# VectorE copies a pair's turned probabilities before it reduces the pair two further on, in the narrow self-attention of a two-layer decoder

## The reference

```python
def _L0_xattn_ref(x, cross_input, Wk, bk, Wq, bq, Wv, bv, ...):
    # C, H = 128, 16; D = C // H = 8; x is the layer norm of the stream
    q = _heads(x @ Wq + bq)
    k = _heads(x @ Wk + bk)
    v = _heads(x @ Wv + bv)
    att = jnp.einsum('bhqd,bhkd->bhqk', q, k) * scale
    causal = jnp.tril(jnp.ones((T, T), bool))
    att = jnp.where(causal[None, None], att, -jnp.inf)
    y = jnp.einsum('bhqk,bhkd->bhqd', jax.nn.softmax(att, axis=-1), v)
    ...            # cross-attention is added to y
    y = y.transpose(0, 2, 1, 3).reshape(x.shape[0], T, C)
    return y @ Wp + bp
```

## Time and profile before

| | |
|---|---|
| runs | 2798.28 us median of 3 (2797.87 to 2806.37) |
| profiled execution | 2795.5 us, of which the span from first to last instruction is 2793.8 us |
| granted TensorE clock, mean of the span | 0.924 |
| busy in the span | PE 2405.5, PEld 1793.3, DVE 2002.1, ACT 1641.1, POOL 1108.5 us |
| busy from 1000 to 1023 us, about one batch of the narrow stage | PE 22.01, PEld 15.18, DVE 18.34, ACT 18.88, POOL 2.94 us |

### The profile page before, as it was taken

One profiled execution on the slowest core, in us unless ns is written; L12 is line 12 of the kernel. 1 busy time (PEld: TensorE's weight loads), 2 busy tenths in 40 slices (PEclk: granted clock), 3 DMA queues, 4 the chain that ended last, 5 costly groups with the idle time before them and its releaser, 6 DMA issues. The chain is left out here.

```text
span 2793.8 us, 48818 instructions
## 1 busy us (share of the span) xinstructions
PE 2405.5 (86%) x16107; PEld 1793.3 (64%) x16107; DVE 2002.1 (72%) x4456; ACT 1641.1 (59%) x4541; POOL 1108.5 (40%) x1577
## 2 busy tenths in 40 slices
PE   5888888887987999979974997999999789998696
PEld 4666666666974666656642774666666567765585
DVE  6999999996335777758979463777776557767565
ACT  6777767772225888866654344777776256654211
POOL 4455785865641111112321312222220155522774
PEclk7999999989997999999986998999999889999798
DMA  8500000004750000000004000000000000000376
GB/s 333 231 1 1 7 10 5 12 7 135 223 159 33 2 2 2 2 16 1 2 1 68 7 1 19 2 1 2 2 1 1 27 1 1 1 1 15 102 225 198
DMA packets 74187, 129.80 MB, mean 46 GB/s; under 512 B 29129, under 2 KB 47633, under 8 KB 69842
## 3 DMA queue, kind: packets, MB, share of 16 engines
q1 hardware_dynamic: 62418, 103.46, 12.3%
q0 software_dynamic: 9216, 19.02, 1.9%
q10 hardware_dynamic: 2304, 4.20, 0.4%
HBM read 69.23 MB, written 57.41 MB: 45 GB/s over the span
## 5 line engine op out<-in xcount | busy, mean ns | idle before, releaser
L1218 DVE TENSOR_TENSOR_SCAN s_state<-s_decay,s_state 128x4096 f32<-128x4096 f32 x32 | 279.0, 8718 | 1.6
L1090 PE MATMUL s_ysumP<-s_state,ident 128*128 128x256 f32 x1024 | 253.6, 395 | 0.0
L2181 ACT ACTIVATE s5a_prob<-s5a_scoreP,s5a_nmax 128x256 f32<-128x256 f32 x512 | 235.5, 481 | 22.7 <-DVE s5a_nmax L2353 21.0
L930 ACT ACTIVATE s_decay<-s_delta,s_aneg 128x255 f32<-128x255 f32 x512 | 211.8, 495 | 53.2 <-POOL s_delta L756 53.0
L2181 ACT ACTIVATE s2s_prob<-s2s_low,s2s_nmax 128x128 f32<-128x128 f32 (+1 forms) x512 | 225.4, 448 | 1.6 <-DVE s2s_nmax L2350 1.6
L1090 PEld LDWEIGHTS s_ysumP<-s_state,ident 128*128 128x128 f32 x1024 | 199.1, 201 | 27.6
L2353 DVE TENSOR_REDUCE s5a_nmax<-s5a_scoreP 128x4 f32<-128x1024 f32 x128 | 156.1, 1220 | 67.3 <-PE s5a_scoreP L2269 65.1
L2350 DVE CUSTOM_DVE_ANT_0 s2s_low<-s2s_scoreP,s2s_mask 128x128 f32<-128x128 f32 (+1 forms) x512 | 151.8, 353 | 55.6 <-PE s2s_scoreP L2269 54.3
L997 PE MATMUL s_bcP<-s_bc,s_sel 96*128 96x256 bf16 x768 | 131.6, 309 | 67.5 <-DVE s_state L1228 49.0
L2364 DVE TENSOR_TENSOR s5a_probT<-s5a_probP,s5a_mask 128x768 f32<-128x768 f32 x128 | 122.5, 957 | 63.1 <-PE s5a_probP L2279 62.0
L1228 DVE TENSOR_TENSOR s_state<-s_state,s_bcP 128x1024 f32<-128x1024 f32 x128 | 149.2, 1215 | 17.5 <-PE s_bcP L997 15.4
(11 more groups left out here) (674 smaller groups left out, 6320.8 us busy)
## 6 DMA issues: line engine op xcount, KB each, us to landing
sorted<-blank SPq DMA_DIRECT2D x32, 1105.0 KB, 27.9
s_state<-in_m_w SPq DMA_DIRECT2D x40, 512.0 KB, 4.2
s5n_m_w<-in_m_w SPq DMA_DIRECT2D x40, 384.0 KB, 3.8
s_decay<-sorted SPq DMA_DIRECT2D x40, 130.0 KB, 2.6
s5n_m_xin<-sorted SPq DMA_DIRECT2D x40, 130.0 KB, 3.2
s4w_mats<-s_scratch SPq DMA_DIRECT2D x4, 1024.0 KB, 13.1
s_state<-parts SPq DMA_DIRECT2D x8, 256.0 KB, 6.7
s_state<-parts ACTq DMA_DIRECT2D x8, 256.0 KB, 7.1
```

What stands on the lines that cost most here:

```text
L930: ins = nc.scalar.activation(decay[c][:, n, 1:], delta[:, c, 1:], ACT.Exp, scale=aneg[:, c, n:n + 1])
L1090: ins = nc.tensor.matmul(ysumP[:, c, :], ident[:], state[s][:, c, n, :], start=False, stop=(n == NS - 1))
L1218: nc.vector.tensor_tensor_scan(cells, flat(decay[c]), cells, 0.0, ALU.mult, ALU.add).then_inc(S["scanned"], 1)
L2181: ins = nc.scalar.activation(prob[i][:, h, a:b], (low[n % 3] if kind == "causal" else scoreP[i])[:, h, a:b], ACT.Exp, bias=nmax[:, p % 4, ...
```

## The change

In VectorE's program, in each iteration of the narrow stage, copy(p-1) is put ahead of maxes(p+1). The reciprocals in iteration 0 come ahead of both. The takes of R0 and L and the statistics stay behind both. For the wide stage, where `LEAD` is false, the order is as it was: maxes(p), reciprocals, copy(p-1), takes.

```diff
             for t, s in batches(ve):
                 st.begin(t)
                 for p in range(PAIRS):
-                    new = following(t, s, p) if LEAD else (t, s, p)
-                    if new:
-                        maxes(*new)
+                    if not LEAD:
+                        maxes(t, s, p)
                     if p == 0 and not first(t):
                         recip(t - 1, 1 - s)
                     e = earlier(t, s, p, 1)
                     if e:
                         turn_out(*e)
+                    new = following(t, s, p)
+                    if LEAD and new:
+                        maxes(*new)
                     at(AT_A, t, s, p, take)
                     at(AT_B, t, s, p, take)
                     if p == 0 and not last(t):
```

## The result

| | before | after |
|---|---|---|
| median of the runs | 2801.01 us (4 runs, 2797.87 to 2806.37) | 2836.06 us (4 runs, 2826.17 to 2844.54) |
| ratio | | 1.0122, 95% interval 1.0084 to 1.0160 |
| profiled execution | 2795.5 us, span 2793.8 | 2844.54 us, span 2842.8 |
| mean granted TensorE clock | 0.924 | 0.912 |

A forecast was written before the change was run, and what follows sets the result against it. TensorE's in-order queue was taken to set the pace. 16.9 us from 14 batches plus 1.25 us from the last make 18.2 us, profiled 2795.5 becoming 2813.7; against the median of 2798.28, forecast 2816.5 us, range 2807 to 2825.

The forecast's parts named there:

- The L take: Narrow stage, iteration 4: VectorE takes L later, so TensorE's Q0 starts 1.21 us late in 14 batches, 16.9 us.
- turn(2): TensorE's transposes of pair 2: wait for the copy goes, later minima make them 0.20 us late, bounds 0 to 0.40.
- The last batch: Narrow stage's end: no ScalarE items cover the minima, three loops of 4.98 us set the pace, 1.25 us more.
- R0: Later take of R0 hidden by 1.1 us before T; rival: T waits, 15.5 us more, 2832 us, chance 0.05.
- The rival of prompt copies: Narrow stage: only TensorE's removed waits for copies count, 5.9 us won, 2792.4 us; chance 0.04.
- that of absorption: Narrow stage: TensorE's idle time takes up 1.0 of 1.21 us per batch, 4.2 us stay, 2802.5 us; chance 0.08.
- The clock: Narrow stage: loss through TensorE's clock left out, as granted clock stayed 1.00 even when TensorE was busy 8.25 of 15 us.

The follow-up runs named there:

- e2: The changed kernel with the take of L ahead of maxes(5) in iteration 4; 2818.69 us median of 10, ratio 1.0055.
- the repetition: The profiled execution of the changed kernel run again without any edit; 2817.24 us, span 2815.5.
- e1: The changed kernel again, with no edit; 2820.86 us median of 9, ratio 1.0098.
- e6: The order of before, with 57 dummy TensorE products at the end of the narrow stage; 2819.27 us median, ratio 1.0074.
- e3: The order of before, with 80 dummy TensorE products at the end of the narrow stage; 2822.45 us median of 6, ratio 1.0081.
- e7: The order of before, with 114 dummy TensorE products at the end of the narrow stage; 2825.76 us median, ratio 1.0099.
- e4: The order of before, with copy(1) ahead of maxes(3) and the take of L ahead of copy(3); 2820.85 us median of 8, ratio 1.0056.
- e9: The order of before, with only the take of L ahead of copy(3); 2812.03 us median of 12, ratio 1.0016.
- e11 to e16: The order of before, moved by 57 dummy products twice more, then by 53, 57, 61 and 65, one execution each; 2803.74 to 2818.54 us.
- e8: The changed kernel with 24 dummy products just ahead of those with `s4w_mats`; 2826.99 us median, ratio 1.0086.
- e10: The changed kernel with 24 dummy products at the end of the narrow stage; 2825.69 us median of 12, ratio 1.0077.

## Why the prediction was wrong

- *The L take: right.* The wait of Q0 appeared 14 times at 1.1 us, the take stands 1.98 behind its copy, and the period is 24.49 us against 24.45. e2 puts the take back and gives back 1.11 us.
- *turn(2): right in the trace, not separately priced.* Its wait for the copy is gone, it waits 0.47 us for exps instead, and the step to it from the scores ahead of it grew from 1.19 (1015.56 to 1016.75 before) to 1.39 us (1006.78 to 1008.17 after), the 0.20 forecast; e2's period, 0.14 above that of before, holds it. The scores of before:

```profile
1015.56 0.92 PE L2269 MATMUL s2s_scoreP<-s2s_k,s2s_q 32*128 32x128 f32 x8
```

- *The last batch: right*, three loops of 4.98 us; some 0.7 us more were lost around them.
- *R0: right.* No wait for its take shows at T. The rival of prompt copies fell, and so did that of absorption: the whole 1.25 us a batch reach the end of the stage, which is 19.0 us longer in the repetition where 18.2 were forecast.
- *The clock: wrong, and this is the step that failed.* "A loss through TensorE's clock I leave out: the granted clock stayed 1.00 even in the stretch where TensorE was busy 8.25 of 15 us". This looked at the changed stage alone. The step "The stage ends at a barrier of all engines, so nothing later hides it" took for granted that the later stages keep their time. They do not: they begin some 20 us later, and in six of 13 runs the time is 18 to 27 us above the middle of the other seven (2817.24); in the traced run of these, 16.8 us lie in 128 products at 1.2 GHz (35.8 against 19.0). The profile of before showed the risk: the clock fell there already, a few microseconds behind these products, and I did not read that stage. So which group a run falls into decides whether the forecast holds: all six lower runs of e1 lie within 2807 to 2825, and of the four of the first measurement none, three being of the upper group.

e6 shows, for the times, that the upper group does not need the new order. That its long runs lose their time through the clock is on record in their mean granted clock; that they lose it in the same products is argued from the 20 us between its groups and the 160.9 us of the three traced blocks against 138.9 to 142.8; no such run was traced. What triggers the fall of the clock stays open. With the order of before, 57 products bring the upper group in 5 of 12 runs, 80 (e3) in none of 6 and 114 (e7) in 1 of 8, and the kernel before unmoved had it or something like it in 5 of 64 (2818 to 2827 us). But the orders of e2, e4 and e9, by whose periods the later stages move by only some 2, 4 and -2 us, have it in 5 of 10, 6 of 8 and up to 6 of 12: that displacement alone sets it off, and the order has no part, is not shown. The start moment alone does not decide (e2, e4 against e11 to e16), and density against moment was not separated (e8, e10).

## What to carry to other kernels

On an in-order engine, a moved wait is priced by what queues behind it and by who needs that: here hardly by the minima, which cost 0.14 us a batch, but by a 0.4 us take that freed a shared bank. An edit in one stage displaces all later ones, and where the clock of TensorE falls close to a block of products, that block can run at half its speed in some executions and not in others, here over 35.8 or 19.0 us; read the granted clock of the later stages too, and split the span by stage before blaming the edit. Where repeated runs fall into two groups, take enough of them to see both, and do not explain a profile from the upper group by the edit.

## What the runs showed of the hardware

The granted clock fell from 1.00 to 0.50 while TensorE was at work almost without a gap: 4.00 of 4.00 us busy in the stretch ahead of the fall, 3.84 in the one in which it fell. It then stayed at 0.50 through 30.00 us in which TensorE and its weight loads were both busy without a pause, most of it in products of 64 columns each with its own 128x128 weights. In the repetition the same instructions, busy for 18.84 of 19.00 us, ran at 1.00 throughout. Going by the Trainium skill (TensorE: Matmul & The Clock Gate, section "What's actually happening"), the lower clock belongs to an idle TensorE and activity releases it. The trace does not agree: busy as the profile counts it did not keep the clock up here, and the measurement decides.
